# Twelve loads per unit moved from SyncE's queue to ScalarE's in an attention and spiking-FFN kernel

## What is computed

```
xn = layernorm(x)
q, k, v = split(xn @ w_qkv);  q, k = irfft(rfft(q) * mask), irfft(rfft(k) * mask)   # per head, 9 frequencies
attn = softmax(q k^T / 4);  a = (attn v) @ w_out + b_out
h = relu(xn @ W_fc^T)^2;  y = h @ W_proj^T
5 steps of: mem = 0.9 mem + y - (mem > 1);  spikes += mem > 1        # f = spikes / 5
out = x + a + f
```

## Time and profile before

| what | value |
|---|---|
| median of 3 runs | 1754.28 us (1751.3 to 1758.28) |
| the profiled execution: its own time | 1755.41 us |
| its span | 1753.6 us |
| mean granted TensorE clock | 0.977 of full speed |
| busy: PE, DVE, ACT, POOL | 93%, 86%, 67%, 45% |
| chain that ended last: PE, DVE, SPq, DMA | 62%, 16%, 13%, 4% |

### The profile page before, as it was taken

The page is one execution under the profiler, slowest core; times in us unless marked ns, Lnnn a source line. Parts: engine busy times, 40 slices in busy tenths (PEclk is TensorE's granted clock), DMA queues, the critical chain, the costliest instruction groups (busy, mean ns, idle before and its releaser), DMA issues.

```text
span 1753.6 us, 60281 instructions
## 1 busy us (share of the span) xinstructions
PE 1634.4 (93%) x24366; PEld 1220.9 (70%) x24366; DVE 1506.6 (86%) x2782; ACT 1177.1 (67%) x2274; POOL 787.4 (45%) x1075
## 2 busy tenths in 40 slices
PE   9998999999999999999899999999999999999898
PEld 6566677677677677777676776776766776767677
DVE  7887898888898889889898898988988888889784
ACT  5546677677676677667676676776776676777572
POOL 2103345555444455555444455554344555544344
PEclk9999999999999999999999999999999999999999
DMA  6761233233222332333222323332223233322423
GB/s 225 231 224 47 69 87 82 66 87 83 80 67 71 84 80 71 83 85 82 68 74 75 84 65 84 85 84 73 68 76 85 70 78 86 83 69 73 134 58 100
DMA packets 150776, 156.83 MB, mean 89 GB/s; under 512 B 74464, under 2 KB 113248, under 8 KB 150496
## 3 DMA queue, kind: packets, MB, share of 16 engines
q1 hardware_dynamic: 147040, 149.75, 31.1%
q10 hardware_dynamic: 3456, 3.21, 0.6%
HBM read 119.80 MB, written 27.79 MB: 84 GB/s over the span
## 4 chain that ended last, share of the span: by engine, by line
PE 62%; DVE 16%; SPq 13%; DMA 4%; issue 3%; ACT 2%; ACTq 0%; POOL 0%; DVEq 0%; POOLq 0%
PE banks L821 22%; PE ring L773 14%; DVE pmax L1032 11%; PE ring L806 10%; PE banks L831 6%; SPq L361 4%; DMA delta_sb<-delta_scratch 4%; PE banks L826 3%; SPq L351 3%; DVE shift L1055 2%; SPq L371 2%; SPq L335 2%; ACT probs L626 2%; PE ring L942 2%; SPq L317 1%
## 5 line engine op out<-in xcount | busy, mean ns | idle before, releaser
L626 ACT ACTIVATE probs<-ring 128x512 f32<-128x512 f32 x2048 | 1076.0, 601 | 485.2 <-PE ring L806 303.7
L1032 DVE TENSOR_REDUCE pmax<-ring 128x1 f32<-128x512 f32 x2000 | 1246.5, 681 | 106.6 <-PE ring L773 98.1
L773 PE MATMUL ring<-kst,qst 64*128 64x512 f32 x2000 | 812.6, 451 | 42.3 <-DVE pmax L1032 42.3
L806 PE MATMUL ring<-qst,delta_sb 64*128 64x512 f32 x1664 | 607.9, 454 | 58.0 <-DMA delta_sb<-delta_scratch 56.4
L821 PE MATMUL banks<-probs,vst 128*32 128x128 f32 x16384 | 564.8, 279 | 0.0
L821 PEld LDWEIGHTS banks<-probs,vst 128*32 128x32 f32 x16384 | 424.1, 111 | 141.9 <-ACT probs L626 99.2
L773 PEld LDWEIGHTS ring<-kst,qst 64*128 64x128 f32 x2000 | 376.8, 188 | 180.2 <-issue 99.8
L806 PEld LDWEIGHTS ring<-qst,delta_sb 64*128 64x128 f32 x1664 | 283.1, 189 | 122.1 <-DMA delta_sb<-delta_scratch 69.8
L826 PE MATMUL banks<-xnT,wfc_sb 64*128 64x128 f32 x2016 | 279.5, 281 | 1.5 <-ACT relu_sb L631 1.5
L826 PEld LDWEIGHTS banks<-xnT,wfc_sb 64*128 64x128 f32 x2016 | 275.2, 197 | 4.9 <-ACT relu_sb L631 1.9
L831 PE MATMUL banks<-wproj_sb,hid_sb 64*128 64x256 f32 x1024 | 263.3, 377 | 0.0
(11 more groups left out here) (97 smaller groups left out, 1113.4 us busy)
## 6 DMA issues: line engine op xcount, KB each, us to landing
kst<-qk_scratch SPq DMA_DIRECT2D x256, 128.0 KB, 2.7
qst<-qk_scratch SPq DMA_DIRECT2D x256, 128.0 KB, 2.9
delta_sb<-delta_scratch SPq DMA_DIRECT2D x256, 64.0 KB, 1.9
tail<-qk_scratch SPq DMA_DIRECT2D x512, 26.0 KB, 2.2
delta_sb<-delta_scratch SPq DMA_DIRECT2D x128, 80.0 KB, 2.1
qk_scratch<-attnT SPq DMA_DIRECT2D x32, 256.0 KB, 3.0
shift_rows<-shiftT SPq DMA_DIRECT2D x512, 2.0 KB
delta_scratch<-tail SPq DMA_DIRECT2D x256, 26.0 KB, 2.0
```

The source lines that it names most:

```text
L626: act.activation(probs[:, g % PS, :], score_bank(g), ACT.Exp, scale=SCALE).then_inc(exp_done, 1)
L773: pe.matmul(max_bank(x), qst[b][rows, tile * P:(tile + 1) * P], kst[b][rows, chunk * BLK:(chunk + 1) * BLK], start=True, stop=True).then_i ...
L806: pe.matmul(score_bank(g), delta_sb[rows, at:at + P], qst[b][rows, q:q + BLK], start=False, stop=True, skip_group_check=True).then_inc(sco ...
L1032: dve.tensor_reduce(pmax[:, tile, chunk:chunk + 1], max_bank(x), AX, ALU.max).then_inc(mx_taken, 1)
```

## The change

`load_delta` moves from SyncE's program to ScalarE's. In the first stage it stands after the first `take_up` and ahead of exp 2, instead of behind the last stores of the first stage on SP. In each of the 31 other cases the four loads of piece 0 stand behind exp 56, the four of piece 1 behind exp 60, and the four of piece 2 behind exp 63 and ahead of `take_up`. The waits are the same as before, now on ScalarE's queue. Late in the program SP gets a wait on `delta_stored` ahead of the load of `wout`.

```diff
-            def load_delta(u, piece):
-
-                cols = slice(*PIECES[piece])
-                src = delta_dram[u % 2, :, :, cols].rearrange("d r t -> (d r) t")
-                sp.wait_ge(delta_stored, STORED * (u + 1))
-                for group in range(4):
-                    sp.dma_start(delta_sb[group * 2 * DH:(group + 1) * 2 * DH, cols].bitcast(F32),
-                                 src).then_inc(delta_in[piece], 16)
...
-            for piece in range(len(PIECES)):
-                load_delta(0, piece)
...
-                if not last:
-                    for piece in range(len(PIECES)):
-                        sp.wait_ge(exp_done, MINI * i + MINI - TB + (piece + 2) * QUAD)
-                        load_delta(i + 1, piece)
...
+            sp.wait_ge(delta_stored, STORED * B * H)
...
+            def load_delta(u, piece):
+
+                cols = slice(*PIECES[piece])
+                src = delta_dram[u % 2, :, :, cols].rearrange("d r t -> (d r) t")
+                act.wait_ge(delta_stored, STORED * (u + 1))
+                if u:
+                    act.wait_ge(exp_done, MINI * (u - 1) + MINI - TB + (piece + 2) * QUAD)
+                for group in range(4):
+                    act.dma_start(delta_sb[group * 2 * DH:(group + 1) * 2 * DH, cols].bitcast(F32),
+                                  src).then_inc(delta_in[piece], 16)
...
+                    if m in (MINI - 8, MINI - 4) and not last:
+                        load_delta(i + 1, (m - MINI) // 4 + 2)
...
                     if m == MINI - 1 and not last:
+                        load_delta(i + 1, 2)
                         take_up(i + 1, 0, UP_A)
...
             take_up(0, 0, UP_A)
+            for piece in range(len(PIECES)):
+                load_delta(0, piece)
```

## The result

The changed kernel takes **1870.58 us** (median of 4 runs, 1868.38 to 1870.76) against 1754.46: a ratio of 1.0658, 95% interval 1.0635 to 1.0681. The forecast was 1826, with a range of 1765 to 1900. The profiled execution took 1870.76 us, its span is 1869.0 us.

The account below looks back on a forecast made before the run. PE, busy 93% of the span, was taken as the bound, waiting most for the key differences (56.4 us). 1755.4 + 60 (unit ends) + 14 (clock) - 3 (first unit) = 1826 us; range 1765 to 1900.

Parts of the forecast that it names:

- The mechanism: At each unit's end, ScalarE's issues delay the relu; a longer wait for it replaces the delta wait: 60 us in all.
- g: Time of a group of four load issues on ScalarE's queue: 1.76 us, range 1.37 to 2.16.
- 3g + 3.14: End of piece 2's issues after exp 56 starts at a unit's end; the relu follows, ending at 9.05 us, against 5.29.
- The clock: After the unit-end stall PE falls to the 1.2 GHz level, losing 1.4 us; ten more units have it, 14 us.
- The first unit: Loads ahead of exp 2 delay PE some 2.4 us, but the 5.5 us wait at L792 goes: together -3 us.
- by itself that is 56 us: Saving at the 31 unit ends from the whole wait for the key differences before score 67 going.
- the fast rival: ScalarE absorbs the issues at the unit's end; delta wait and 5.5 us go: about 1694 us, chance 0.09.
- the forecast's sign: Whole kernel slower, chance 0.85, against 0.09 for faster and 0.06 for the same.
- PE's wait at the relu: At PE L826, a wait for the relu replaces the one for the differences, 31 times, 3 to 4 us.
- 3g - 3.34: Extra cost of each of 31 unit ends: 1.94 us, with 0.77 and 3.14 us as the ends of the range.
- the third rival: At the unit's end one wait replaces another of its size: within 0.5%, 1746 to 1764 us, chance 0.06.
- The hindering of the queues: ScalarE's first two groups sit out SyncE's issues: 6.6 us more a unit, 205 us, about 1971 us; chance 0.07.

Follow-up runs that it names:

- Swapping one line: Changed kernel with the relu of the unit's end put ahead of the four loads of piece 2 on ScalarE: 1784.9 us, 1.0141.
- keeping PE at work: Changed kernel with the matmul pair of first score 65 done six times over in the stall, only the last signalling: 1817.5 us, 1.0358.
- keeping SyncE quiet: Changed kernel with SyncE's four loads of keys and four moves of the output held back until exp 63 is done: 1854.5 us, 1.0561.

## Why the prediction was right, and where its terms were off

- **The mechanism held.** The relu stands behind three groups of issues, the first `share` waits for it, and PE stands there 31 times. Swapping one line gives 86 us back; the waits without issues cost nothing in the kernel before. The size was too small: the whole came to 115 us in the profiled executions, 1870.8 against 1755.4, where I had 71.
- **The relu came later than forecast.** I took g = 1.76 us for a group. In the unit shown the three groups take 2.14, 2.14 and 1.83 us from the first issue to the next activation, 6.11 in place of 5.28 (the mean is 6.05). An issue measured 0.44 us at the median where I had taken 0.40, and SyncE's issues beside the second group add 0.36. With 0.24 us of small gaps that I had left out, the relu came at 9.49, not at 3g + 3.14 = 8.42. Over the 31 ends it starts 4.99 us later than before, where I had 3.76: 38 us in all, the largest error.
- **The clock** was undersized too: 14 us for ten more units. Between the relu and exp 67 it costs 4.04 us against 4.67 - 1.82 = 2.85 before without its wait, 1.19 us a unit. From exp 67 to exp 72 a unit gets 0.23 back. That is 0.96 us a unit or 30 us. The 53 us that keeping PE at work gave is another difference: it holds also the clock that the kernel before had lost behind its own stall.
- **The terms together**, by the unit: the relu 4.99 later, the wait of 1.82 gone, the clock 0.96, and 0.28 less in the rest of the unit, where SyncE is no longer late for the maxima. That is 3.86 us with rounding, in 31 units 120, and 4 less in the first unit: 115.
- **The first unit** was forecast at -3 us. Exp 3 comes 4.1 us later there, not 2.4, since piece 0 is in place for PE only at 122.0 us, not at 119.2; but the wait of 5.5 us for the maxima is gone, and exp 56 comes 4.2 us earlier.
- **What the waits for the differences are worth.** They are gone as said. But "by itself that is 56 us" leaves out the lower clock behind each of them, though I had its price in hand, 1.4 us a unit in two units of three. With it the relief is worth 107 us, and the fast rival would stand near 1650 us, not at 1694. Loads moved earlier on SyncE bring none of it, because the wait comes back at step 32. This didn't move the forecast's sign, since the relief has nothing to act on while PE waits for the relu: SyncE then idles, 12 us a unit and not the 6 that I gave.
- **PE's wait at the relu** was forecast at 3 to 4 us and is 2.4 on the mean. In the unit shown PE reaches it 2.4 us later than before (768.42 - 2.27 - 758.28 = 7.87 us behind exp 56, against 5.46), held up by the late exponentials of the last two quads. The delay was as real, but only a part of it shows under that name.
- **Two readings of mine were weak.** The activation at 27.20 in the earlier trace rows, from which I took that an issue holds the queue, is put down there to a wait for VectorE, so that row alone didn't show it; the 1.9 us ahead of the relu, put down to "issue", do. And by my own 3g - 3.34 a g of 1.0 to 1.3 us gives -10 to +17 us, not all of it within the 0.5% of the third rival.
- **The hindering of the queues.** The first stage's rows had let me think of none. It is there, 16 us in all as measured by keeping SyncE quiet, and a long way from the 205 us of that rival. The Trainium skill ("Perfetto Trace Analysis", DMA Instruction — HWDGE) has one descriptor generator shared by two sequencers and locked for exclusive use while an issue's descriptors are made. If the lock lasted for the whole of an issue, each would wait one of the other queue out; the second group's 2.20 us with SyncE beside it and 1.84 without bear out no more than a small part of that, and the first group shows nothing of it.

How the 16 us of the queues split into longer issues and the clock behind them wasn't measured by itself.

## What to carry to other kernels

A DMA issue takes its queue's time, and a compute engine's queue is free for it only while the next instruction couldn't start anyway. Measured against the kernel without these loads (1650 us), twelve issues a unit cost 17 us with one behind each exponential, 33 with two, and 221 with four in a row ahead of an instruction that the bounding engine waits for. So look at what stands behind the issues on their queue, and who waits for it.

When an issuing queue has no idle time left, moving its last load up only moves the wait. Taking issues off the queue is worth the wait and the lower clock behind it, here 57 and 42 us. Both when an idle time on TensorE comes and when one goes, the lower clock behind it is to be counted.

## What the runs showed that I had not expected

- 0.35 to 0.44 us of issue runs wholly beside an activation of 0.60 us, and the exponentials keep their 0.49 us from start to start.
- Beside SyncE's loads of keys piece 0 lands 3.9 us after its issue at the median, without them 2.1 us. No wait hangs on it in the later units.
- PE with more work in its idle time took 53 us less than the changed kernel.
